# Token rows of an expert layer: one transposed form from TensorE, the exchanged form copied by ScalarE

## The reference, cut to what matters

```python
xn = layernorm(x)                                   # x: 4 x 1024 x 128
out = x + attention(xn, Wq, bq, Wk, bk, Wv, bv, Wo, bo) + experts(xn)
# attention: 16 heads of 8 dimensions, softmax over 1024 keys
# experts: 8 of them; per token the two with the largest logits,
#   h = silu(xt @ w_gate[e]) * (xt @ w_up[e]);  out += g[e] * (h @ w_down[e])
# w_gate, w_up: 128 x 256, w_down: 256 x 128, all float32
```

## Time and profile before

| what | value |
|---|---|
| median of 3 runs | 877.51 us (877.37 to 879.19) |
| profiled execution | 878.5 us, its span 876.8 us |
| TensorE matmul busy | 823.2 us (94%) |
| VectorE busy | 741.4 us (85%) |
| ScalarE busy | 694.7 us (79%) |
| GpSimd busy | 474.0 us (54%) |
| mean granted TensorE clock | 0.971 |

### The profile page before, as it was taken

The page is one execution under the profiler, slowest core; times in us unless marked ns, Lnnn a source line. Parts: engine busy times, 40 slices in busy tenths (PEclk is TensorE's granted clock), DMA queues, the critical chain, the costliest instruction groups (busy, mean ns, idle before and its releaser), DMA issues.

```text
span 876.8 us, 20205 instructions
## 1 busy us (share of the span) xinstructions
PE 823.2 (94%) x6745; PEld 442.0 (50%) x6745; DVE 741.4 (85%) x1381; ACT 694.7 (79%) x1520; POOL 474.0 (54%) x670
## 2 busy tenths in 40 slices
PE   7997765799999999999999999999999999999997
PEld 6754222244555555555555565555555555555532
DVE  6589998978989878989888978898988878989834
ACT  3551553668889989989888988898988888988886
POOL 8141035013666656657666656676766756666510
PEclk8997787999999999999999999999999999999999
DMA  5877059022343333343443323334334334342233
GB/s 147 182 227 232 2 122 55 25 70 58 67 103 82 79 85 69 98 93 88 98 94 87 94 66 94 84 70 98 77 94 97 82 96 95 85 93 63 40 92 108
DMA packets 94824, 80.92 MB, mean 92 GB/s; under 512 B 19560, under 2 KB 84320, under 8 KB 94688
## 3 DMA queue, kind: packets, MB, share of 16 engines
q1 hardware_dynamic: 80080, 67.18, 30.0%
q0 software_dynamic: 13632, 11.79, 8.9%
q10 hardware_dynamic: 1008, 0.66, 0.4%
HBM read 58.51 MB, written 22.71 MB: 93 GB/s over the span
## 4 chain that ended last, share of the span: by engine, by line
PE 83%; DVE 12%; issue 2%; ACT 2%; DMA 1%; ACTq 0%; DVEq 0%
PE ps L1139 27%; PE ps L1124 17%; PE ps L1114 15%; PE ps L1186 7%; DVE maxima L919 7%; PE ps L1169 6%; PE ps L1152 2%; PE ps L1025 2%; ACT probs L631 1%; PE ps L1175 1%; DVE xnT L901 1%; PE ps L1202 1%; PE ps L1036 1%; PE ps L1146 1%; PE ps L1030 1%
## 5 line engine op out<-in xcount | busy, mean ns | idle before, releaser
L919 DVE TENSOR_REDUCE maxima<-ps 128x1 f32<-128x512 f32 x1024 | 637.7, 684 | 77.2 <-PE ps L1124 72.0
L631 ACT ACTIVATE probs<-ps 128x512 f32<-128x512 f32 x1024 | 537.6, 608 | 113.1 <-PE ps L1114 110.5
L1124 PE MATMUL ps<-qk 64*128 64x512 f32 x1024 | 406.2, 447 | 38.4 <-DVE maxima L919 37.7
L1114 PE MATMUL ps<-qk 64*128 64x512 f32 x1024 | 375.2, 456 | 2.1 <-ACT probs L631 1.4
L1124 PEld LDWEIGHTS ps<-qk 64*128 64x128 f32 x1024 | 186.4, 188 | 181.3 <-DVE maxima L919 150.1
L1139 PE MATMUL ps<-probs,v_all 128*9 128x512 f32 x2048 | 271.1, 602 | 1.7 <-ACT o_sb L637 1.1
L1114 PEld LDWEIGHTS ps<-qk 64*128 64x128 f32 x1024 | 179.5, 188 | 22.8 <-ACT probs L631 13.5
L526 POOL DMA_INDIRECT acc<-result,idx x71 | 117.6, 1657 | 113.3 <-issue 89.0
L1186 PE MATMUL ps<-xg_T,gu_w 64*128 64x128 f32 x1136 | 155.4, 276 | 0.0
L1186 PEld LDWEIGHTS ps<-xg_T,gu_w 64*128 64x128 f32 x1136 | 145.6, 187 | 8.3 <-ACT result L658 8.1
L1169 PEld LDWEIGHTS ps<-dn_w,hid 64*128 64x128 f32 x568 | 73.5, 186 | 70.8 <-ACT probs L631 51.5
(11 more groups left out here) (150 smaller groups left out, 619.0 us busy)
## 6 DMA issues: line engine op xcount, KB each, us to landing
gu_w<-L_ffn_w_gate SPq DMA_DIRECT2D x71, 128.0 KB
gu_w<-L_ffn_w_up SPq DMA_DIRECT2D x71, 128.0 KB
dn_w<-L_ffn_w_down SPq DMA_DIRECT2D x71, 128.0 KB
qk<-q_parts SPq DMA_DIRECT2D x126, 64.0 KB
qk<-k_parts SPq DMA_DIRECT2D x126, 64.0 KB
k_parts<-stage SPq DMA_DIRECT2D x23, 256.0 KB, 3.4
q_parts<-stage SPq DMA_DIRECT2D x16, 256.0 KB, 3.4
x_sb<-L_attn_inputs SPq DMA_DIRECT2D x4, 512.0 KB, 7.9
```

Of the source, the lines that this page charges most:

```text
L631: act.activation(probs[:, u % NPB, q, h, :], ps[:, BANK_OF[job], :], ACT.Exp).then_inc(s_read, 1)
L919: dve.tensor_reduce(maxima[:, p % 2, qt, h, k:k + 1], ps[:, x_bank(i), :], AX.X, ALU.max, negate=True).then_inc(x_read, 1)
L1114: pe.matmul(ps[:, bank, :], t[r, 1, kt * P:(kt + 1) * P], t[r, 0, q * CH:(q + 1) * CH], start=True, stop=True).then_inc(s_filled, 1)
L1124: pe.matmul(ps[:, bank, :], t[r, 0, qt * P:(qt + 1) * P], t[r, 1, k * CH:(k + 1) * CH], start=True, stop=True).then_inc(x_filled, 1)
```

## The change

Only the plain form of the rows is turned on TensorE: one transpose per half, piece 2, in place of two. ScalarE makes the exchanged form, by two copies of 64 partitions each that read the upper 64 partitions of PSUM into the lower ones of `xg_T` and the other way round. The gathered row shrinks to 132 numbers, written by one transfer in place of three. In the hand-written order `("max", 0, 0)` now stands ahead of `("piece", 1, 0)`, the one that waits for half 0; `("score", 0, 1)` stands ahead of `("piece", 1, 1)`.

```diff
-RW = E + 64 + 4
-ROWS_DOWN = (("piece", 0, 0), ("score", 1, 0), ("piece", 0, 1), ("max", 1, 0), ("piece", 0, 2), ("score", 1, 1), ("piece", 0, 3),
-             ("max", 1, 1), ("score", 0, 0), ("piece", 1, 0), ("max", 0, 0), ("piece", 1, 1), ("score", 0, 1),
-             ("piece", 1, 2), ("max", 0, 1), ("piece", 1, 3))
+ROWS_DOWN = (("piece", 0, 0), ("score", 1, 0), ("piece", 0, 1), ("max", 1, 0), ("piece", 0, 2), ("score", 1, 1),
+             ("max", 1, 1), ("score", 0, 0), ("max", 0, 0), ("piece", 1, 0), ("score", 0, 1), ("piece", 1, 1),
+             ("max", 0, 1), ("piece", 1, 2))
...
-        rows_dram = dram("rows", [P + T, RW], F32)
+        rows_dram = dram("rows", [P + T, XW], F32)
...
-        xg = sb("xg", [P, 4, RW])
+        xg = sb("xg", [P, 4, XW])
...
-                    for to, n, first in ((0, E, 0), (E, 64, 0), (E + 64, 4, E)):
-                        sp.dma_start(rows_dram[P:P + T, to:to + n].rearrange("(n p) e -> p n e", p=P),
-                                     x_sb[:, :, first:first + n]).then_inc(rows_stored, 16)
+                    sp.dma_start(rows_dram[P:P + T, :].rearrange("(n p) e -> p n e", p=P), x_sb[:, :, :]).then_inc(rows_stored, 16)
...
-            pool.wait_ge(rows_stored, 64)
+            pool.wait_ge(rows_stored, 32)
...
-                    ins = act.activation(xg_T[:, c % 2].rearrange("p k n -> p (k n)"), ps[:, BANK_OF[job], 0:2 * P], ACT.Copy)
+                    act.activation(xg_T[:, c % 2, 0, :], ps[:, BANK_OF[job], 0:P], ACT.Copy)
+                    for h in range(2):
+                        ins = act.activation(xg_T[64 * h:64 * h + 64, c % 2, 1, :],
+                                             ps[64 - 64 * h:128 - 64 * h, BANK_OF[job], 0:P], ACT.Copy)
...
-                    ins = act.activation(result[:, t % 3, :], ps[:, BANK_OF[job], 2 * P:2 * P + E], ACT.Copy, scale=gate[:, t % 4:t % 4 + 1])
+                    ins = act.activation(result[:, t % 3, :], ps[:, BANK_OF[job], P:P + E], ACT.Copy, scale=gate[:, t % 4:t % 4 + 1])
...
-                    first, last = (0 if c >= 2 else 2), (3 if c < USED else 1)
+                    first, last = (0 if c >= 2 else 2), (2 if c < USED else 1)
...
-                        mm = pe.matmul(ps[:, bank, k * P + 64 * h:k * P + 64 * h + 64], xg[r, c % 4, 64 * k:64 * k + P], ident[r, r],
+                        mm = pe.matmul(ps[:, bank, 64 * h:64 * h + 64], xg[r, c % 4, 0:E], ident[r, r],
                                        start=(h == 0 and part == first), stop=(h == 1 and part == last), is_transpose=True)
```

More of the change, by code:

```diff
@@ L214, in build @@
         tile_e = early[:, 8 * NT * NE:8 * NT * NE + TILES * NE].rearrange("p (t e) -> p t e", e=NE)
-        zeros = early[:, 2688:2688 + RW]
-        idx_f = early[:, 2688 + RW:2688 + RW + TILES]
+        zeros = early[:, 2688:2688 + XW]
+        idx_f = early[:, 2688 + XW:2688 + XW + TILES]
         iota_i = sb("iota_i", [P, P], I32)
@@ L501, in gate_of @@
                     pool.wait_ge(s_read, s_taken("rows", t - 2))
-                pool.tensor_scalar(gate_is[:, 0, :], xg[:, s, E + 64:E + 66], tile_f[:, t:t + 1], None, ALU.is_equal).then_inc(gate_step, 1)
+                pool.tensor_scalar(gate_is[:, 0, :], xg[:, s, E:E + 2], tile_f[:, t:t + 1], None, ALU.is_equal).then_inc(gate_step, 1)
                 pool.wait_ge(gate_step, 2 * t + 1)
-                pool.tensor_tensor(gate_is[:, 1, :], gate_is[:, 0, :], xg[:, s, E + 66:E + 68], ALU.mult).then_inc(gate_step, 1)
+                pool.tensor_tensor(gate_is[:, 1, :], gate_is[:, 0, :], xg[:, s, E + 2:E + 4], ALU.mult).then_inc(gate_step, 1)
                 pool.wait_ge(gate_step, 2 * t + 2)
@@ L692, in take_proj @@
                     act.wait_ge(rows_ready, 4)
-                    act.wait_ge(rows_stored, 64)
+                    act.wait_ge(rows_stored, 32)
                     act.wait_ge(idx_ready, 1)
@@ L1168, in expert_part @@
                             pe.wait_ge(hid_ready, t + 1)
-                        mm = pe.matmul(ps[:, bank, 2 * P:2 * P + E], hid[r, s, part * P:(part + 1) * P], dn_w[r, s, part, :],
+                        mm = pe.matmul(ps[:, bank, P:P + E], hid[r, s, part * P:(part + 1) * P], dn_w[r, s, part, :],
                                        start=(h == 0 and part == 0), stop=(h == 1 and part == last))
                     else:
-                        k = part - 2
-                        if (h, part) == (0, 2):
+                        if h == 0:
                             pe.wait_ge(xg_in[c % 4], 16 * (c // 4 + 1))
-                        mm = pe.matmul(ps[:, bank, k * P + 64 * h:k * P + 64 * h + 64], xg[r, c % 4, 64 * k:64 * k + P], ident[r, r],
+                        mm = pe.matmul(ps[:, bank, 64 * h:64 * h + 64], xg[r, c % 4, 0:E], ident[r, r],
                                        start=(h == 0 and part == first), stop=(h == 1 and part == last), is_transpose=True)
```

## The result

The changed kernel takes 909.4 us (median of 4 runs, 907.0 to 911.1) against 877.4 for the kernel before: a ratio of 1.036 (95% interval 1.033 to 1.039), 32 us slower. The profiled execution's span is 909.3 us, before it was 876.8. The forecast was 885, its range ended at 892: the sign was right, the size was too small by a factor of four.

The account below looks back on a forecast made before the run. The prediction took rows units to be bound by a loop through VectorE's reduction and gate units by ScalarE's result copy. Profiled 878.5 plus 7.5 us gave 886.0, less 1.0 for the median 885.0; range 876 to 892.

Parts of the forecast that it names:

- The bound of the rows unit: Rows unit: a loop of 1.95 us through VectorE, whose first reduction frees the bank for the last maximum.
- Transposes and order: Rows unit: dropping 2 of 4 transposes and moving maximum and score gain 0, at a cost of at most some hundredths.
- today's wait: Gate unit: its first expert piece waits for ScalarE's result copy, costing only 0.05 us per unit but using up the slack.
- TensorE is the bound: Rival: TensorE's own queue sets the rows unit's last maximum; each rows body falls to 1.76 us, total 871.5; chance 0.14.
- the cover: Rows unit: VectorE's reduction hides the removed transposes; without it at most 0.19 us per unit could be won.
- The price of a delay: Gate unit: each further delay of the result copy is paid in full, 0.21 us in each of 34 units.
- ScalarE's copies: ScalarE: one 256-column copy becomes three of 128 columns, 0.16 us each; 0.47 against 0.26, so the result copy ends 0.21 later.
- the forecast's own sum: Gate units: 34 x 0.21 = 7.1 us plus 9 x 0.04 = 0.4, together +7.5 us.
- the 9 split units: Gate units with a split of maxima inside: VectorE holds the last maximum, covering up to some 0.28 us more delay.
- Hidden: ScalarE elsewhere: 71 x 0.21 = 15 us more load, claimed to add no time to gate or `up` units.
- 0.26 each (no shorter than 256 columns): ScalarE: upper limit for the spacing of the three copies, making the delay of the result copy +0.53 us.
- Small copies are not shorter: Rival: ScalarE's three copies take 0.26 us each, a delay of 0.53, total about 902 us; chance 0.10.

Follow-up runs that it names:

- e1: The changed kernel with its two exchange copies made over all 128 partitions, unshifted, one into xg_T and one into a spare tile: 887.2 us, ratio 1.0095.

## Why the prediction was wrong in size

**What held.** The bound of the rows unit was read rightly: the last maximum's weights wait for the first reduction. Transposes and order were costed at 0; the two alone, with the exchange for nothing, bring 3 us, and the early release gives the same 3 us to the kernel before. Both traces put 1.8 to 1.9 of them in the gate units, where today's wait had been priced at 34 x 0.05 = 1.7; the rest can't be told from scatter. The order alone brings nothing. The rival "TensorE is the bound", resting on 199 of 200 us busy and on the 17.2 us of idle loads, is refuted by the run without exchange copies and by this one. But the cover was thinner than the forecast had it: it allowed 0.19 us per rows unit if VectorE's reduction went, and with the maximum first the body fell by 0.02 only.

The price of a delay was right too: "Every further delay of the copy is paid in full". Unit 95 got its piece 0.60 later and became 0.61 longer. At full height, a delay of 0.21 (0.24 with the longer result copy) cost 9.5 us against 7.5 forecast.

**What failed** is one term: *ScalarE's copies*, "128 columns give 0.16. Three are 0.47", and its assumption "I take 64 partitions to cost as much as 128". The slope by columns was right (0.157 measured at full height). Nor is a short copy dearer in itself: it lasts 0.27 us where the one of 128 partitions lasts 0.31. What the term took for granted is that each copy overlaps with its neighbour. But the short copies start at partition 64 on one side and 0 on the other, and an ACTIVATE whose first partition differs from its predecessor's waits for that one to end. Every ACTIVATE of the kernel before reads and writes from partition 0, so its trace could not show this. The three spacings became 0.32, 0.29 and 0.28, 0.89 in all, the delay 0.60 after the 0.03 that the result copy is shorter, in place of 0.21. Put into the forecast's own sum: 34 x 0.60 = 20.4; the 9 split units, covered for 0.28, pay 0.32 each, 2.9; the 16 behind `turn_shift` pay by how early their copy ended, 5.8 in all by the trace: 29 us of the 32.

"Hidden", said of ScalarE's load elsewhere, held at the forecast delay and not at the real one: at 0.60 the gate unit's first exponential ends 0.13 us later. In the changed kernel the late piece covers this; with the early release it is what is left, 11.6 us in the gate units by the trace.

**The bound failed with it.** "0.26 each (no shorter than 256 columns)" took the dearest spacing in the trace for the ceiling. A spacing is a duration less an overlap; without overlap the ceiling is the duration, about 0.3 us. Three of them make 0.9, which is what came. The rival "Small copies are not shorter" came nearest, at 902, but by another mechanism: it had the spacing of the old copy, not the loss of the overlap.

By the Trainium skill (ScalarE: Activation LUTs, section What ACT_TABLE_LOAD costs) ACTIVATEs one behind the other overlap by about 93 ns. The traces do not agree: the full-height copies of 128 columns (run e1) overlap by 0.15 us and more, and copies whose first partition changes by nothing.

**Not separated:** 32 us at the median against 29 in the sum. By the traces the units with expert work hold 29.4 of the 32.5 us between the spans; some 2 lie behind the last store's issue and 1.1 ahead of unit 28, and no run was made for these.

## What to carry to other kernels

When one instruction is cut into several short ones, cost them at their full duration unless the trace shows neighbours of exactly that form overlapping; the overlap of the old form is the first thing that a cut can lose. Work moved off a busy engine wins nothing where that engine only looks busy: find out who releases the last instruction of the loop, here a VectorE reduction 0.05 us ahead of it. And a semaphore raised by the last of several operations of an engine should be raised by the one that is really needed: that alone made the kernel before 0.3% faster (875.0 us), the best version of this study together with the one that adds the new order.

## What was new of the hardware

On ScalarE, an ACTIVATE begins 0.01 us behind the end of its predecessor when the first partition that it reads or that it writes differs from the predecessor's, and otherwise 0.1 to 0.2 us before that end. Full height behind full height: starts 0.16 apart with 128 columns. Half behind full height, both from partition 0: 0.16. Half behind half, both reading 64 and writing 0: 0.18. With a change on either side: 0.27 to 0.32, the whole duration of the one ahead. This holds in all 71 tiles of the changed kernel and of each of the three kernels with copies of 64 partitions, 0.011 to 0.013 us behind the end; in the changed kernel with the early release one such pair lies 0.025 apart, where the first of the two raises a semaphore. Other changes than between 0 and 64 were not tried, and why the engine does this is not shown.
